# Moving two value-projection tiles behind the first scores of an attention layer

## The reference, cut to what matters

```
hn  = group_norm(x) * scale + bias
qkv = w_qkv @ hn + b_qkv            # q, k, v of 8 heads, 64 channels each
wgt = softmax((q*s).T @ (k*s))      # 1024 x 1024 for each head
a   = wgt @ v
out = x + group_norm(w_proj @ a + b_proj)
```

## Time and profile before

| what | value |
|---|---|
| median of 3 runs | 3598.97 us |
| lowest and highest run | 3598.38 and 3599.15 us |
| span of the profiled execution, first to last instruction | 3596.4 us |
| own time of the profiled execution | the span; what lies around it in a run is 2.6 us by the median |
| PE busy | 3475.9 us, 97% of the span |
| DVE, ACT, POOL busy | 2104.1, 1828.4, 994.2 us |
| mean granted TensorE clock | 0.984 |

### The profile page before, as it was taken

One profiled execution on the slowest core, in us unless ns is written; L12 is line 12 of the kernel. 1 busy time (PEld: TensorE's weight loads), 2 busy tenths in 40 slices (PEclk: granted clock), 3 DMA queues, 4 the chain that ended last, 5 costly groups with the idle time before them and its releaser, 6 DMA issues.

```text
span 3596.4 us, 52422 instructions
## 1 busy us (share of the span) xinstructions
PE 3475.9 (97%) x17296; PEld 2845.8 (79%) x17296; DVE 2104.1 (59%) x3363; ACT 1828.4 (51%) x3082; POOL 994.2 (28%) x891
## 2 busy tenths in 40 slices
PE   7999999989999899998999989999999999999999
PEld 3887788878888788887878878788787887888878
DVE  4677446774378634786347854478444774447742
ACT  3577226761278522784237832388223882247812
POOL 0234103440034300352114521045111451114411
PEclk9999999999999999999999999999999999999999
DMA  7622215312234113331033211342203422142210
GB/s 278 180 45 65 91 38 139 78 41 82 65 112 95 48 59 95 86 91 71 36 118 83 71 71 42 112 95 60 82 36 106 95 60 82 39 135 62 59 47 24
DMA packets 63519, 294.41 MB, mean 82 GB/s; under 512 B 9200, under 2 KB 9456, under 8 KB 52464
## 3 DMA queue, kind: packets, MB, share of 16 engines
q1 hardware_dynamic: 63216, 290.65, 27.6%
HBM read 158.49 MB, written 31.46 MB: 53 GB/s over the span
## 4 chain that ended last, share of the span: by engine, by line
PE 86%; issue 7%; DVE 3%; ACT 2%; POOL 1%; DMA 0%; ACTq 0%; SPq 0%; DVEq 0%; POOLq 0%
PE big L419 36%; PE tps L516 14%; PE big L543 12%; PE ops L529 12%; PE ops L658 10%; DVE XA L1163 1%; PE ops L419 1%; ACT PB L784 1%; PE big L581 1%; POOL XA L912 1%; DVE HL L1284 0%; DVE small L1104 0%; PE big L635 0%; PE ops L624 0%; ACT RB L801 0%
## 5 line engine op out<-in xcount | busy, mean ns | idle before, releaser
L902 POOL TENSOR_SCALAR PB<-PB,small 128x1024 f32<-128x1024 f32 x576 | 647.9, 1125 | 1334.5 <-DVE small L1110 1328.6
L790 ACT ACTIVATE PT<-tps 128x512 fp32r<-128x512 f32 x1088 | 601.1, 597 | 249.4 <-PE tps L516 246.0
L1115 DVE TENSOR_TENSOR PT<-tps,PT 128x512 fp32r<-128x512 f32 x1088 | 692.7, 678 | 38.6 <-ACT PT L790 38.6
L419 PE MATMUL big<-HH,W 128*128 128x512 f32 x1856 | 618.2, 404 | 61.8 <-DVE HL L1284 56.5
L1104 DVE TENSOR_REDUCE small<-big 128x1 f32<-128x1024 f32 x512 | 624.7, 1220 | 62.5 <-PE big L543 59.2
L516 PE MATMUL tps<-ident,PB 128*128 128x128 f32 x4608 | 617.4, 275 | 8.4 <-DVE PT L1115 6.1
L516 PEld LDWEIGHTS tps<-ident,PB 128*128 128x128 f32 x4608 | 527.6, 140 | 122.0 <-DVE PT L1115 52.5
L784 ACT ACTIVATE PB<-big,small 128x1024 f32<-128x1024 f32 x512 | 572.2, 1117 | 73.1 <-DVE small L1104 70.2
L529 PE MATMUL ops<-PT,VT 128*128 128x512 f32 x2048 | 599.1, 414 | 0.0
L543 PE MATMUL big<-ST 128*128 128x512 f32 x2048 | 555.2, 393 | 10.9 <-ACT PB L784 10.9
L419 PEld LDWEIGHTS big<-HH,W 128*128 128x128 f32 x1856 | 361.8, 195 | 149.2 <-issue 70.9
(11 more groups left out here) (130 smaller groups left out, 3669.9 us busy)
## 6 DMA issues: line engine op xcount, KB each, us to landing
ST<-ST SPq DMA_DIRECT2D x384, 256.0 KB, 5.0
W<-d_qk SPq DMA_DIRECT2D x32, 1024.0 KB, 5.5
XA<-in_x SPq DMA_DIRECT2D x8, 2048.0 KB, 8.9
X<-in_x SPq DMA_DIRECT2D x8, 2048.0 KB, 10.4
W<-d_wp SPq DMA_DIRECT2D x8, 2048.0 KB, 12.1
W<-d_g SPq DMA_DIRECT2D x8, 2048.0 KB, 12.1
W<-d_m SPq DMA_DIRECT2D x8, 2048.0 KB, 7.8
W<-d_u SPq DMA_DIRECT2D x8, 2048.0 KB, 7.6
```

The lines of the kernel that those rows point to most:

```text
L419: last = mm(dst, stat(sp_, k), mov(mp_, k), start=(i == 0), stop=(i == n - 1))
L790: act_fn(pt_slot(u, s)[:, 0, :], tps[n % 2][:], ACT.Copy).then_inc(s_pt_hi, 1)
L902: nc.gpsimd.tensor_scalar(PB[:, i, :], PB[:, i, :], rinv[:, i:i + 1], 1.0, ALU.mult, ALU.mult)\
L1115: V.tensor_tensor(pt_slot(u, s)[:, 1, :], tps[n % 2][:], pt_slot(u, s)[:, 0, :].bitcast(f32), ALU.subtract).then_inc(s_pt_ready, 1)
```

## The change

`project_v(1)` moves into step 0 and `project_v(2)` into step 2, each behind that step's score tile; the two single tiles move from steps 0 and 3 to steps 3 and 4. `BIG` and the programs of ACT and DVE follow. Nothing is computed differently, and no instruction is added or taken away, apart from register work. SP's program is the same, though its wait for both single tiles (`v_full`), behind which the weights of head pairs 2 and 3 are loaded, now ends with step 4.

```diff
 def last_values(step):
-    return {0: NT - 2, 3: NT - 1}.get(step)
+    return {3: NT - 2, 4: NT - 1}.get(step)
+
+def late_values(step):
+    return {0: 1, 2: 2}.get(step)

-BIG = [("qk", j) for j in range(4)] + [("v", i) for i in range(3)]
+BIG = [("qk", j) for j in range(4)] + [("v", 0)]
 for _step in range(STEPS0):
     if qk_part(_step) is not None:
         BIG.append(("qk", qk_part(_step)))
     BIG.append(("s", _step))
+    if late_values(_step):
+        BIG.append(("v", late_values(_step)))
...
                 pe.wait_ge(s_ld_wv, b * 16 + 16)
-                for i in range(3):
-                    project_v(i)
+                project_v(0)
...
                     if step < STEPS0:
                         scores0(u, tb)
+                    if late_values(step):
+                        project_v(late_values(step))
                     if last_values(step):
                         project_last_v(last_values(step))
...
                     if step < STEPS0:
                         exps(u, tb)
+                    if late_values(step):
+                        v_hi(late_values(step))
                     if last_values(step):
                         last_v_hi(last_values(step))
...
                     if step < STEPS0:
                         row_max(u, tb)
+                    if late_values(step):
+                        v_lo(late_values(step))
                     if last_values(step - 1):
                         last_v_lo(last_values(step - 1))
```

More of the change, by code:

```diff
@@ L810, in body @@
                     qk_hi(j)
-                for i in range(3):
-                    v_hi(i)
+                v_hi(0)
                 for step in range(STEPS0 + LAG):
@@ L1119, in body @@
                     qk_lo(j)
-                for i in range(3):
-                    v_lo(i)
+                v_lo(0)
                 for step in range(STEPS0 + LAG):
```

## The result

The changed kernel takes 3689.55 us (median of 4 runs, 3687.8 to 3690.35) against 3598.98 us before: a ratio of 1.0252, 95% interval 1.0238 to 1.0267. It is 90.6 us slower. The profiled executions differ by just as much, 3687.0 against 3596.4 us, so the traces hold the whole difference. The granted clock is the share of full speed that the profile shows for TensorE; its mean over the profiled execution went from 0.984 to 0.978.

What follows compares the result with a forecast made beforehand. TensorE, busy for 97% of the span, was taken to set the end. Stack copies 52.3, steps 0 to 5 8.0, step 6 4.8 and clock falls 20 and 16 sum to 101 us: 3700 us from 3599, range 3660 to 3726.

Steps and rivals of the forecast that it cites:

- the uncovered copies: Ahead of each image's first score tile TensorE waits for six stack copies: 6.1 us, 9.6 in the first image; 52.3 us.
- the open chain: Steps 0 to 5: value tile 1's buffer release lacks cover before value tile 2; net 1.0 us an image, 8.0 in all.
- step 6: Last single tile's low part on VectorE delays the first transposed tile's: 0.6 us more wait an image, 4.8 us.
- the first fall of the clock: Behind the wait for the stacks the granted clock falls in every image, 2.5 us each: 20 us.
- a second fall in every image: Behind the two 1.4 us pauses after value tile 1 the clock falls again, 2.0 us each: 16 us.
- the first rival: No second clock fall, the two pauses about a score tile being taken as work: 3684 us; chance 0.25.
- My bound from below: Wait for the stacks could be nothing: last q and k result out at 536.0, a single copy landing 5.3 us later.
- the 1.9 us that I called idle: Steps 0 to 5 before the change: 14.64 us holding 12.7 us of matmuls, the rest idle and fillable.
- the 2.9 of the new order: Idle us between value tiles 1 and 2 in the new order: a 4.7 us chain less 1.8 us of matmuls.
- the four costs that I averaged: Earlier clock falls, priced at half their work at 0.50: 1.45, 3.0, 1.65 and 4.0 us, 2.5 on average.
- the case that fell: Earlier trace from 793.70: TensorE busy 0.80 of 2.30 us and the clock fell; the new stretch judged nearer to it.
- that which held: Earlier trace from 557.10: TensorE busy 2.15 of 3.4 us and the clock held at 1.00.

Runs made afterwards that it cites:

- 5.4 us more cover: Changed kernel with value tile 1 back ahead of the first score tile, tile 2 still in step 2: 3622.83 us, ratio 1.0065.
- the single tiles alone: Kernel before with only the single value tiles moved, from steps 0 and 3 to steps 3 and 4: 3615.1 us, ratio 1.0043.
- useless matmuls: Changed kernel plus 26 matmuls nobody reads between value tile 0 and the wait for the stacks: 3673.79 us, ratio 1.0209.
- a single tile ahead: Changed kernel with single value tile 6 (12 matmuls) moved from step 3 ahead of the first score tile: 3673.99 us, ratio 1.0209.
- GpSimd's copies: Changed kernel with three of the six copies into the first stack made by GpSimd instead of the DMAs: 3648.08 us, ratio 1.0133.

## Why the prediction was right, and where it was off

The direction, the place and the range (3660 to 3726) were right, and so were four of the five terms: the uncovered copies, the open chain, step 6 and the first fall of the clock. The fifth, a second fall in every image, did not come. 3689.55 is 10 us below the forecast and nearest to the first rival, 3684, to which I had given half the chance of the forecast; its mechanism, no second fall, is what happened in seven images of eight.

- **Wait for the stacks: 52.3 forecast, 53.8 measured.** In seven images it was 5.9 us where 6.1 was forecast. The first image waited 12.5, not 9.6: its copies were issued from 102.42 us on, against 99.70 before. SyncE waits for the setup's last store there: it was issued at 93.52 us against 91.98, and the weights' load behind it 8.4 us later against 7.2. The trace that I read was the exception: in all nine others these copies were issued between 100.68 and 102.81 us. With all three value tiles ahead such a lateness is mostly hidden (1.4 and 1.8 us of wait in the first image of two experiments); here it reaches the end whole. With 5.4 us more cover the first image waited 6.4 us, with 2.7 more 8.4. My bound from below was misread, too: 5.3 us is the time of the sixth copy, issued behind five others; the first lands 2.9 us after its issue.
- **Steps 0 to 5: 8.0 forecast, 9.7 measured**, with both pauses where they were expected, 1.47 us for L1092 and 1.2 for L792. The experiment with the single tiles alone shows that the chain is a matter of what stands behind a value tile. Of the 1.9 us that I called idle before, only 0.21 + 1.15 = 1.36 are pauses in the earlier trace rows; the 2.9 of the new order was counted in the same way, so their difference stands.
- **Step 6: 4.8 forecast, 4.8 measured.**
- **First fall of the clock: 20 forecast, 19.5 measured.** It fell in each image. Half of the work at 0.50 behind the waits is 19.5 us. Of the four costs that I averaged, the 1.45 is half of the 2.90 us of work in the row from 802.85 of the earlier trace rows. The useless matmuls price it in seven images at 16.3 us, 2.3 each; in the first, the 12.5 us wait left 3.74 us of work at 0.50, 1.9 us. The closeness to 20 is in part luck: the single falls cost 1.5 to 3.1 us, and the four that I averaged 1.45 to 4.0.

```profile
115.56:119.30 3.74, 3.74 (x9) 2.97 (x10) 1.22 (x1) 0.38 (x1) 0.00 (x0) 0.50 1.03 232
```

- **Second fall: 16 forecast, in one image of eight, 3.30 / 2 = 1.7 us measured.** This is the term that was mis-sized. I had put the stretch with two pauses of 1.4 us nearer to the case that fell, with 0.80 us busy of 2.30, than to that which held, with 2.15 of 3.40. The stretch came as I had read it, with TensorE busy for 2.06 us of the 4.70 from 574.20. The step that failed is the one from there to a fall in every image: the clock held in seven of eight, as it did at 557.10. Nor is it never: the same two pauses, 1.47 and 1.17 us about a score tile, brought a fall in two images of eight with the single tiles alone, in three with a single tile ahead, and in none with the useless matmuls or with GpSimd's copies. A chance in each image should have been priced, not all or nothing. What decides in which image it falls is open.
- **Not in the forecast:** layer 1 did not stay unchanged. TensorE waited 2.7 us more there for L1180, in three images instead of one. The traces show when: in the images where the clock rose sooner behind the long pause in layer 1. These are the second image, without the wait, and the third, with it:

```profile
825.90:832.70 6.80, 2.75 (x6) 1.82 (x6) 6.21 (x7) 2.77 (x4) 4.96 (x4) 0.50 0.27 116
832.80:839.60 6.80, 5.99 (x15) 4.72 (x15) 6.67 (x6) 1.91 (x2) 3.61 (x2) 0.50 0.10 11
1276.50:1283.20 6.70, 2.90 (x6) 1.82 (x6) 6.11 (x6) 3.03 (x4) 5.22 (x4) 0.50 0.19 81
1283.40:1290.10 6.70, 4.86 (x20) 3.76 (x21) 6.70 (x6) 1.55 (x2) 3.26 (x2) 1.00 0.09 15
```

```profile
1288.22 0.49 PE L426 MATMUL big<-HH,W 128*128 128x512 f32 x1 [1.33 <-DVE PB L1180]
```

In all ten traces this wait stands in just the images whose clock rose sooner there, one in the kernel before, three here, none to five in the experiments. It is what TensorE meets when it gets there earlier, and no loss: from the restart in layer 1 to the end of the next image's first value tile, the third image took 176.8 us and the second 178.1. No experiment forces it, so that it is the clock is read from the traces alone.

The terms' errors, measured less forecast: +1.5 for the copies, +1.7 for steps 0 to 5, 0 for step 6, -0.5 for the first falls, -14.3 for the second. About 1 us is left for the setup and layer 1.

## What to carry to other kernels

Before work is moved to fill idle time, ask what it covers where it stands: here the matmuls of three value tiles, 16.3 us, hid copies that are not complete until 11.3 us after the last q and k matmul (5.44 + 5.89), and two of the tiles were taken away for 1.9 us of idle time. A transfer that is waited for nowhere in the profile can still be the nearest bound, and the time from its landing to its user is read from its issue row and its time to landing. Where a buffer's release needs two engines in turn, put work on another buffer behind it, before that buffer's next use: with the single tile there 0.21 and 1.15 us were idle, without it 1.47 and 1.17.

## What the runs showed of the hardware

Useless matmuls through a DMA wait made a kernel faster by 15.8 us, 0.4%, because the granted clock stayed at 1.00. Behind a pause of 1.9 us the clock fell in four of seven images, behind 3.2 us in four of seven, and behind 5.9 us in all seven; in the second image TensorE had been busy through the whole 10.0, 9.9 and 10.0 us ahead of these three pauses. Two pauses of 1.47 and 1.17 us about a score tile brought a fall in none to three images of eight. And a GpSimd copy of 64x1024 from fp32 to fp32r within the on-chip memory took 2.75 us, while its scaled copies of 128x1024 in fp32 take 1.1 us each; which of the differences between the two makes it, no run here tells.
